# Making the second chunk's tile table at the chunk boundary instead of in the middle of the first chunk, in two routed mixture-of-experts layers

## The reference

```
logits = xt @ w_gate                                  # 4096 tokens, 8 experts
top_logits, sel = top_k(logits, 2)
probs = softmax(top_logits)
h = silu(einsum('td,edh->eth', xt, w1)) * einsum('td,edh->eth', xt, w3)
y = einsum('eth,ehd->etd', h, w2)                     # hidden width 256
out = sum over the two chosen experts of probs * y
```

## Time and profile before

| | |
|---|---|
| median of 3 runs (2613.54 to 2620.45) | 2617.51 us |
| the profiled execution's own time | 2617.51 us |
| its span, first to last instruction | 2615.7 us |
| time around the span | 1.8 us |
| busy share of TensorE, VectorE, ScalarE, GpSimd | 83%, 63%, 49%, 54% |
| mean granted TensorE clock | 0.897 of full speed |

### The profile page before, as it was taken

The page is one execution under the profiler, slowest core; times in us unless marked ns, Lnnn a source line. Parts: engine busy times, 40 slices in busy tenths (PEclk is TensorE's granted clock), DMA queues, the critical chain, the costliest instruction groups (busy, mean ns, idle before and its releaser), DMA issues. The chain is left out here.

```text
span 2615.7 us, 40507 instructions
## 1 busy us (share of the span) xinstructions
PE 2182.7 (83%) x11776; PEld 1307.4 (50%) x11776; DVE 1654.8 (63%) x4436; ACT 1285.1 (49%) x2268; POOL 1425.0 (54%) x1403
## 2 busy tenths in 40 slices
PE   4577898999879979989999974786899999974786
PEld 3344565666755656654444433454444444433454
DVE  6865775776567757766666653434788777853434
ACT  4543453332435543326666632443577667752443
POOL 5933754443346543436666645664666766615664
PEclk8778898999778989999999986898999999985788
DMA  1000110222011112220000021133000000021124
GB/s 50 0 3 18 46 42 20 104 98 73 13 35 33 38 60 97 89 96 1 1 1 1 1 72 58 57 96 105 1 1 1 2 2 1 1 67 55 56 84 143
DMA packets 106957, 112.58 MB, mean 43 GB/s; under 512 B 21816, under 2 KB 86200, under 8 KB 106488
## 3 DMA queue, kind: packets, MB, share of 16 engines
q1 hardware_dynamic: 97656, 91.08, 11.9%
q0 software_dynamic: 9088, 18.89, 2.1%
HBM read 71.91 MB, written 25.29 MB: 37 GB/s over the span
## 5 line engine op out<-in xcount | busy, mean ns | idle before, releaser
L2332 DVE TENSOR_REDUCE l_diffneg_max<-psum 128x1 fp32r<-128x512 f32 x512 | 335.2, 685 | 92.2 <-PE psum L2070 84.0
L2247 ACT ACTIVATE l_diffweights<-psum 128x1024 f32<-128x1024 f32 x256 | 261.8, 1025 | 132.1 <-PE psum L2099 131.0
L2070 PE MATMUL psum<-l_diffkz,l_diffQ 128*128 128x512 f32 (+1 forms) x512 | 234.8, 477 | 3.2 <-DVE l_diffneg_max L2332 2.1
L2871 ACT ACTIVATE l_lightswapped<-psum 32x512 f32<-32x512 f32 x304 | 178.7, 588 | 101.4 <-DVE l_lightturned L2963 98.0
L5050 POOL DMA_INDIRECT results<-l_moe1y,l_moe1xt x156 | 149.8, 960 | 128.7 <-DVE l_moe1y L4970 109.9
L1597 DVE TENSOR_REDUCE l_attn0neg_max<-psum 128x1 fp32r<-128x512 f32 x256 | 167.3, 683 | 53.3 <-PE psum L1328 50.4
L1503 ACT ACTIVATE l_attn0weights<-psum 128x1024 f32<-128x1024 f32 x128 | 130.2, 1022 | 117.4 <-PE psum L1350 117.3
L1724 POOL TENSOR_TENSOR l_attn0half_sums<-l_attn0weights 128x2048 f32<-128x2048 f32 x30 | 137.1, 4571 | 88.6 <-ACT l_attn0weights L1503 88.6
L4296 ACT ACTIVATE l_moe0s<-psum 128x512 f32<-128x512 f32 x144 | 85.7, 595 | 198.2 <-PE psum L855 177.0
L4717 PE MATMUL psum<-l_moe1w,l_moe1zt 128*128 x312 | 181.5, 667 | 0.0
L4733 PEld LDWEIGHTS psum<-l_moe1w,l_moe1gt 128*128 128x128 f32 x624 | 93.9, 205 | 162.2 <-issue 162.2
(11 more groups left out here) (602 smaller groups left out, 6012.2 us busy)
## 6 DMA issues: line engine op xcount, KB each, us to landing
l_moe0bcs<-gate_rows SPq DMA_DIRECT2D x64, 512.0 KB, 4.0
l_moe1xt<-sorted SPq DMA_DIRECT2D x156, 66.0 KB, 1.8
l_attn0Q<-l_attn0q_hi SPq DMA_DIRECT2D x128, 64.0 KB, 2.0
l_moe1yb<-results SPq DMA_DIRECT2D x32, 256.0 KB, 3.1
l_moe1w<-in_moe_w SPq DMA_DIRECT2D x6, 1024.0 KB, 8.0
l_attn0Q<-l_attn0q_lo SPq DMA_DIRECT2D x64, 64.0 KB, 2.0
l_moe0w_raw<-in_moe_w SPq DMA_DIRECT2D x20, 128.0 KB, 4.7
results<-l_moe1y,l_moe1xt POOLq DMA_INDIRECT x156, 2.2
```

Of the source, the lines that this page charges most:

```text
L2070: nc.tensor.matmul(ps[:, bank, :], Q[rows, n % 4, st * P:(st + 1) * P], kz[rows, n % 4, hh, :], start=True, stop=True).then_inc(pe_max.sem ...
L2247: nc.scalar.activation(weights[:, tt, 2 * pair:2 * pair + 2, :], ps[:, S[m % 2]:S[m % 2] + 2, :], ACT.Exp, scale=SCALE).then_inc(act_exp.s ...
L2332: nc.vector.tensor_reduce(neg_max[:, n % 2, st, row:row + 1], ps[:, bank_of(("max", n, b)), :], AXX, ALU.max, negate=True).then_inc(vec_ma ...
L2871: copy = lambda to, frm: nc.scalar.activation(to, frm, ACT.Copy)
```

## The change

The call of `tabled(c)` is taken out of `prepare` and put at the head of the loop over chunks in VectorE's list. For chunk 0 that is the same place. For chunk 1 it is behind all 41 turns of chunk 0. Inside `tabled`, the copy that makes "pads" moves from the first place to the last. Since "pads" is now the last step, three waits change: SyncE's wait for "row" goes (its wait for "pads" ahead of the pad writes covers it), TensorE waits for "pads" where it waited for "row", and VectorE's own wait ahead of resetting `run` is for "pads" instead of "count".

```
             sp.wait_ge(padded[c], 16 * 8)
-            wait(sp, vec_table, c, "row")
...
         expert_of = lambda i: t.value_load(...)
-        wait(t, vec_table, c, "row")
+        wait(t, vec_table, c, "pads")
...
                 if j:
-                    wait(d, vec_table, chunk_of(j) - 1, "count")
+                    wait(d, vec_table, chunk_of(j) - 1, "pads")
...
             wait(d, chooser.vec_gate, last_of(c), "comb")
-            inc(v.tensor_copy(table[:, c, PAD_AT:PAD_AT + 8], run[:, :]), "pads")
             inc(v.tensor_tensor(count[:, :], run[:, :], base[:, :], ALU.subtract), "count")
...
             inc(v.tensor_scalar(table[:, c, ROW_AT:...], at_row[:, 0:many], ...), "row")
+            inc(v.tensor_copy(table[:, c, PAD_AT:PAD_AT + 8], run[:, :]), "pads")
...
                 placed(due(c, k, 9))
-                if due(c, k, 9) == last_of(c):
-                    tabled(c)
...
         for c in range(R.CHUNKS):
             n0 = R.FIRST_TILE[c]
+            tabled(c)
             for i in turns(c):
```

## The result

The changed kernel took 2653.17 us (median of 4 runs, 2647.09 to 2657.81), the kernel before 2618.98 us (median of 4, 2613.54 to 2620.61). That is 34 us slower; 2654.8 us were forecast. Eleven runs of the changed kernel are on record in all (2640.30 to 2657.81, median 2648.60 us), and the ratio over these is 1.012, 95% interval 1.0094 to 1.0147, that is 31 us, between 25 and 38. For the kernel before there are 47 with those beside the experiments (2611.23 to 2638.60, median 2621.72 us; one more, of 4067.58 us, lies far outside and is left out): 27 us between the medians. So the change costs about 30 us, and the medians of four runs leave that open by several. The profiled execution took 2655.23 us with a span of 2653.5 us, 37.8 us more than before.

A forecast was written before the change was run, and what follows sets the result against it. The chain table, eight pad writes, tile load, transpose, first result, hidden at the chunk boundary, was expected to come into the open: 36.7 + 5.3 - 4.7 = 37.3 us on 2617.5 gives 2654.8 us, range 2645 to 2663.

The forecast's parts named there:

- The table behind the last copy opens the chain: Chunk boundary, layers 7 and 9: table, pad writes, tile load, transpose, first y lie exposed; 19.2 and 17.5, together 36.7 us.
- restart: Chunk boundary, from first transpose of chunk 1 to its first copy of y: 7.0 us taken.
- Low clock at the restart: Both boundaries: after some 18 us idle TensorE starts at the lower clock; had it stayed up, 3.9 us less.
- Start of chunk 0: Pads copy ends 3.47 us later; 2.9 us exposed in layer 7, 2.4 in layer 9, together 5.3 us.
- What comes back in chunk 0: Turn 27: the table no longer holds up a y copy and GpSimd; 2.5 and 2.2, together 4.7 us gained.
- SyncE late anyway: Boundary: SyncE reaches chunk 1's pads late, so a later table costs only what exceeds this slack; 2618 us; chance 0.04.
- Slow restart: Boundary: clock stays low or tiles refill at chunk 0's pace, 13.5 us a layer, 27 in all; 2682 us; chance 0.06.
- Relief: Chunk 0: taking the table out gives back more than the boundary costs, 26.5 us a layer; 2606.5 us; chance 0.02.
- Sum: Both layers: boundaries 36.7 plus chunk 0 starts 5.3 less 4.7 won back, 37.3 us slower.

The follow-up runs named there:

- pads-last: Kernel before with only the pads copy moved to the end of the table, and its waits; 2620.09 us, ratio 1.0005.
- early pads: Kernel before with chunk 1's eight pad writes put two behind each of chunk 0's last four tile loads; 2619.44 us, ratio 0.9990.
- turn 34: Kernel before with the table of chunk 1 moved from turn 27 to turn 34 of chunk 0; 2618.51 us, ratio 0.9999.
- turn 37: Kernel before with the table of chunk 1 moved to turn 37 of chunk 0, pads copy first; 2633.78 us, ratio 1.0047.

## Why the prediction was right

- **The table behind the last copy opens the chain: right.** By its own terms, layer 7 then layer 9, measured against forecast: table behind the end of the copy 3.46 and 3.47 (3.64), to the first pad write 0.75 and 0.75 (1.11), pads 8.32 and 8.35 (8.42, 8.70), to the tile load 2.10 and 2.10 (2.27, 2.39), to the transpose 1.79 and 1.90 (1.82, 1.88), restart 6.83 and 6.79 (7.0). The boundaries cost 18.2 + 16.1 = 34.3 us instead of 36.7; nearly every term was a little too long (the last but one of layer 9 was not), the first pad write most. TensorE idled 16.7 and 16.9 us, where about 18 were forecast.
- **Low clock at the restart: right, and shown.** The restart is 6.8 us with an idle TensorE and 5.0 to 5.3 when it is kept busy up to its start. By the rule of the Trainium skill ("TensorE: Matmul & The Clock Gate", Part 1) both boundaries start at the low level, and the trace agrees: the mean clock over the two restarts is 0.66 and 0.65. Unforeseen was that the kernel before is itself at the edge: the kernels that keep a covered boundary had restarts of 5.0 to 7.9 us and gaps of 5.2 to 9.1.
- **Start of chunk 0: right.** 2.7 + 2.0 = 4.7 us against 5.3, and the pads-last kernel has it alone.
- **What comes back in chunk 0: near in size, with a part that has another cause.** 4.7 us were forecast, and the two profiles show 3.35 + 3.34 = 6.7. Over the five kernels with the table at the boundary, chunk 0 took 114.3 us on average (ten values of the column above), over before and pads-last 116.7 (four values): 2.4 us a layer, 4.8 in all; with early pads, whose table stands in turn 27 too, it is 1.9 a layer, 3.7 in all. So 4.7 is met no closer than by a microsecond or two. To the y of tile 26, where the table stood, the changed kernel is faster by 1.5 and 3.0 us, and GpSimd issues the store of that result in layer 7 after 0.30 us of idle time instead of 2.83: that is the mechanism of the forecast. The rest of layer 7 lies in the last six tiles, which take 15.27 us before and 13.34 after. The next fence is this stretch before, the one behind it the same stretch after:

```profile
1720.10:1735.37 15.27, 10.86 (x43) 6.66 (x42) 3.69 (x12) 3.94 (x11) 11.45 (x12) 0.78 0.34 102
```

```profile
1715.25:1728.59 13.34, 8.51 (x45) 5.17 (x43) 3.68 (x11) 4.36 (x13) 10.09 (x11) 1.00 0.19 61
```

  The instructions are nearly the same in number; the clock is 0.78 before and 1.00 after. The pad writes that run beside this stretch before (DMA share 0.34) are no cause by themselves: with the pads copy last only, they run there too, and layer 7 took 13.35 us at a clock of 1.00. Why the clock fell in one and not in the other stays open. In turn 34 these tiles had such a clock too.
- **Rivals.** SyncE late anyway: it asks for the pads only 1.8 us behind the y of tile 32, which is the cover that turn 34 still has and turn 37 has not; in the changed kernel the pads come 16 us later than that. Slow restart: none beyond 8.4 us. Relief: 2.4 us a layer, not 21.
- **Sum.** 34.3 + 4.7 - 6.7 - 0.2 (first transpose to first y of chunk 0) = 32.1 us against 37.3; the profiles differ by 5.7 more, and the medians by 34.2 over four runs each, the eleven runs by 31. That the four runs came within 2 us of 2654.8 is in part luck. The 0.1% allowed for single executions was too little as well: the 47 runs before range from 0.4% below their median to 0.6% above it.

## What to carry to other kernels

A small step that waits for nothing can still be the head of a long chain on other queues. Before moving it, write down when its consumer would ask for it: here nothing is lost until that point, and past it every microsecond of lateness is lost. A queue that issues from registers needs about a microsecond a DMA (8.3 us for eight here), so the chain behind a table is longer than its transfers. And when a move wins something on the engine that it leaves, see over several executions whether the gain is the move's or the clock's.

## What the runs showed that was not expected

Single executions of one kernel scatter by some 20 us (27 over the 47 runs before), and the profiles show that much in a layer that no experiment touched. Layer 8, between the two routed layers, took 509.8 to 527.0 us in ten profiles, one of each kernel, 510.0 in that of before and 521.8 in the changed one. Busy time over this layer, before and then after (the stretches are cut to whole microseconds):

```profile
1822.00:2332.00 510.00, 488.45 (x2808) 230.30 (x2808) 384.49 (x737) 344.38 (x408) 316.33 (x320) 0.98 0.01 3
```

```profile
1834.00:2355.00 521.00, 502.19 (x2808) 236.29 (x2808) 384.65 (x737) 344.37 (x407) 316.43 (x320) 0.95 0.01 3
```

TensorE's 2808 matmuls are busy 14 us longer and its weight loads 6 us, the other engines to 0.2 us as long as before, and the clock is 0.95 instead of 0.98. Why it is lower in some executions stays open. So stage times taken from timelines decided the questions of 2 to 5 us here, and the medians could not.
